# A decoder layer's software pipeline: a new table of stage order per engine and of shared PSUM banks

## What is computed

```python
x = x + _L0_attn_ref(_layernorm(x, axis=-1), L0_attn_W_attn, L0_attn_b_attn, L0_attn_W_proj, L0_attn_b_proj)
x = x + _L0_xattn_ref(ctx_1024, ctx_1024, _layernorm(x, axis=-1), ...)
x = x + _L0_ffn_ref(_layernorm(x, axis=-1), ...)
# attention: softmax(mask(q k^T / sqrt(8))) v, q and k scaled by a rope factor
# ffn:
rw, sel = jax.lax.top_k(softmax(x @ router_w.T), 2)
h = jax.nn.silu(g) * u                  # per expert, F = 256
y = jnp.einsum('etf,efd->etd', h, w_down)
out = jnp.einsum('te,etd->td', cw, y) + gate * shared
```

## Time and profile before

| what | us |
|---|---|
| median of 3 runs | 505.77 (505.45 to 506.39) |
| profiled execution, its own time | 505.77 |
| span of the profiled execution | 503.9 |
| outside the span | 1.87 |
| PE busy | 441.4, 88% of the span |
| DVE busy | 357.6, 71% |
| ACT busy | 294.3, 58% |
| POOL busy | 200.1, 40% |

### The profile page before, as it was taken

How to read it: one execution, slowest core, us unless ns; L and a number is a source line. 1 busy time by engine, 2 the same in 40 slices (tenths; PEclk the granted TensorE clock), 3 DMA queues, 4 the chain that set the end, 5 groups by cost and what they waited for, 6 DMA issues and landing times.

```text
span 503.9 us, 13713 instructions
## 1 busy us (share of the span) xinstructions
PE 441.4 (88%) x4508; PEld 298.5 (59%) x4508; DVE 357.6 (71%) x1236; ACT 294.3 (58%) x951; POOL 200.1 (40%) x247
## 2 busy tenths in 40 slices
PE   4868899999989989999999997678988889989993
PEld 3323555655556556556565555456777777777783
DVE  4573677888888798797886957794666666656585
ACT  1125678878778787778687865521444444444520
POOL 7702030031443432432323255550555555555471
PEclk9999999999999999999999997588999999999998
DMA  7600001101011011111111016121332223221294
GB/s 198 178 13 23 29 9 33 36 29 40 19 51 51 19 50 52 34 51 35 50 45 31 24 56 207 43 82 37 85 82 77 77 76 85 75 79 58 64 345 129
DMA packets 41604, 34.69 MB, mean 69 GB/s; under 512 B 6464, under 2 KB 36432, under 8 KB 41536
## 3 DMA queue, kind: packets, MB, share of 16 engines
q1 hardware_dynamic: 36478, 24.51, 17.1%
q0 software_dynamic: 4320, 8.99, 5.3%
q10 hardware_dynamic: 738, 0.33, 0.2%
HBM read 17.26 MB, written 12.09 MB: 58 GB/s over the span
## 4 chain that ended last, share of the span: by engine, by line
PE 64%; DVE 16%; issue 9%; ACT 5%; another core or an unknown queue 2%; SPq 1%; POOL 1%; DMA 1%; ACTq 0%; DVEq 0%; POOLq 0%
PE ps_scores L855 7%; PE ps_scores L677 6%; PE ps_shared L863 5%; PE ps_scores L706 5%; PE ps_shared L872 4%; PE ps_shared L723 4%; PE ps_shared L660 3%; PE ps_scores L684 3%; PE ps_shared L773 3%; DVE negmax L1158 3%; PE ps_scores L809 3%; PE ps_scores L702 3%; DVE vst L1357 2%; PE ps_scores L711 2%
## 5 line engine op out<-in xcount | busy, mean ns | idle before, releaser
L610 POOL DMA_INDIRECT ys<-ctx_t,xload x71 | 68.7, 968 | 69.4 <-ACT ctx_t L1044 51.0
L949 ACT ACTIVATE probs<-ps_scores 128x512 f32<-128x512 f32 x128 | 69.7, 608 | 14.7 <-PE ps_scores L711 14.7
L597 POOL TENSOR_TENSOR x1b<-x,bias 128x128 f32<-128x128 f32 x32 | 14.4, 450 | 160.6 <-DVE x L1179 160.6
L591 POOL DMA_INDIRECT xs<-xrow,posu x64 | 63.8, 997 | 27.4 <-DVE rsum L1280 13.7
L855 PE MATMUL ps_scores<-wide,xe 128*128 x213 | 68.3, 430 | 0.8 <-DVE xe L1352 0.8
L945 ACT ACTIVATE s_copy<-ps_scores 128x512 f32<-128x512 f32 x64 | 38.4, 605 | 31.5 <-PE ps_scores L684 31.5
L1363 DVE COPY probs<-ps_shared 128x256 f32<-128x256 f32 x71 | 30.1, 424 | 37.6 <-PE ps_shared L863 25.6
L1034 ACT ACTIVATE xe<-ps_scores 128x128 fp32r<-128x128 f32 x71 | 19.8, 278 | 51.0 <-PE ps_scores L847 34.8
L1158 DVE TENSOR_REDUCE negmax<-ps_scores 128x4 f32<-128x512 f32 x64 | 41.3, 685 | 10.5 <-PE ps_scores L684 9.9
L872 PE MATMUL ps_shared<-wd,probs 128*128 x284 | 43.9, 277 | 0.3 <-DVE probs L1363 0.3
L677 PE MATMUL ps_scores<-wide,qk 32*128 32x512 f32 x256 | 38.4, 671 | 2.9 <-ACT probs L949 2.6
(11 more groups left out here) (219 smaller groups left out, 1035.5 us busy)
## 6 DMA issues: line engine op xcount, KB each, us to landing
xload<-xs SPq DMA_DIRECT2D x71, 66.0 KB
wide<-qk SPq DMA_DIRECT2D x64, 64.0 KB
wide<-ys SPq DMA_DIRECT2D x8, 512.0 KB, 8.4
ctx_t<-in_ctx SPq DMA_DIRECT2D x32, 64.0 KB, 1.9
out_x<-res SPq DMA_DIRECT2D x8, 256.0 KB, 3.1
ys<-ctx_t,xload POOLq DMA_INDIRECT x71
wd<-in_L_ffn_w_down SPq DMA_DIRECT2D x8, 128.0 KB, 3.2
xs<-xrow,posu POOLq DMA_INDIRECT x64
```

The costliest lines, as they stand in the source:

```text
L591: pool.indirect_dma_start(out=xs, out_offset=bass.IndirectOffsetOnAxis(ap=posu[:, g % 2, k, u:u + 1], axis=0), in_=xrow[:, g % 2, k, u, :] ...
L610: pool.indirect_dma_start(out=ys, out_offset=bass.IndirectOffsetOnAxis(ap=xload_i[:, i % XL, C + 1:C + 2], axis=0), in_=ybuf[:, i % 4, :], ...
L949: act.activation(probs[:, b % 2, j * HJ:(j + 1) * HJ, :].rearrange("p a t -> p (a t)"), SC[score_bank(("scores_t", b), j)][:], ACT.Exp)\
```

## The change

The tables `ORDER` and `BANK` get other contents, and one wait goes. No stage's own code is changed, except that DVE's statistics of the next group no longer wait for the former ones, which the same engine made (lines behind 1074 have one number less after the change).

```diff
 ORDER = {
     "SP": [
-        ("project", 14, 1, 0),
-        ("turn_x2", 10, None, None),
-        ("project", 16, 0, 0),
-        ("turn_max", 14, None, None),
+        ("project", 26, 1, 0),
+        ("turn_x2", 18, None, None),
+        ("turn_max", 25, None, None),
+        ("project", 27, 0, 0),
...
     "DVE": [
...
+        ("xout", -5, None, None),
+        ("row_max", 1, 1, None),
...
-BANK = {"turn_xprobs": 1, "turn_x": 0, "turn_y": 0, "xproject": 3, "attn_out": 3, "values": 1, "xscores": 3, "turn_ffn": 2, "xout": 2, "turn_max": 2, "project_v": 0, "tall_sums": 1, "router": 2,
+BANK = {"turn_xprobs": 2, "turn_x": 3, "turn_y": 2, "xproject": 0, "attn_out": 3, "values": 3, "xscores": 1, "turn_ffn": 3, "xout": 2, "turn_max": 2, "project_v": 2, "tall_sums": 1, "router": 0,
...
-                w.ge(x_stats, g)
```

More of the change, by code:

```diff
@@ L72 @@
     "PE": [
-        ("scores", -3, None, None),
-        ("turn_ffn", -10, None, None),
-        ("xscores", -8, None, None),
-        ("turn_y", -6, None, None),
-        ("values", -5, None, None),
-        ("xout", -9, None, None),
-        ("turn_x2", -7, None, None),
-        ("scores_t", -4, None, None),
-        ("router", -10, None, None),
-        ("attn_out", -6, None, None),
-        ("project_v", -1, None, None),
-        ("tall_sums", -5, None, None),
-        ("project", 0, 0, 0),
@@ L86 @@
-        ("ranks", -14, None, 0),
-        ("gate_up", -42, None, None),
-        ("xproject", -7, None, None),
-        ("project", 0, 1, 0),
-        ("turn_x", 1, None, 0),
-        ("turn_max", -3, None, None),
-        ("turn_xprobs", -8, None, None),
+        ("turn_max", -5, None, None),
+        ("scores", -4, None, None),
+        ("xout", -10, None, None),
+        ("turn_ffn", -11, None, None),
+        ("xscores", -9, None, None),
+        ("turn_x2", -8, None, None),
+        ("turn_y", -7, None, None),
@@ L93 @@
+        ("values", -6, None, None),
+        ("scores_t", -5, None, None),
+        ("project_v", -2, None, None),
+        ("router", -11, None, None),
+        ("attn_out", -7, None, None),
+        ("gate_up", -42, None, None),
+        ("tall_sums", -6, None, None),
+        ("turn_xprobs", -9, None, None),
+        ("ranks", -15, None, 0),
+        ("turn_x", 0, None, 0),
+        ("xproject", -8, None, None),
+        ("project", -1, 0, 0),
+        ("project", -1, 1, 0),
     ],
     "ACT": [
+        ("rstd_x", 2, None, 0),
@@ L95 @@
+        ("turn_x2", -8, None, None),
+        ("route", -15, None, 0),
+        ("turn_y", -7, None, None),
+        ("values", -6, None, None),
         ("xscores", -9, None, None),
-        ("turn_x2", -8, None, None),
         ("rstd_ffn", -10, None, None),
         ("exps", -5, 0, None),
+        ("project_v", -2, None, None),
         ("exps", -5, 1, None),
-        ("project_v", -2, None, None),
         ("exps", -5, 2, None),
+        ("turn_xprobs", -9, None, None),
         ("exps", -5, 3, None),
@@ L163 @@
 W_LOADS = 15
-BANK = {"turn_xprobs": 1, "turn_x": 0, "turn_y": 0, "xproject": 3, "attn_out": 3, "values": 1, "xscores": 3, "turn_ffn": 2, "xout": 2, "turn_max": 2, "project_v": 0, "tall_sums": 1, "router": 2, "turn_x2": 0, "ranks": 0, "project": (2, 0)}
+BANK = {"turn_xprobs": 2, "turn_x": 3, "turn_y": 2, "xproject": 0, "attn_out": 3, "values": 3, "xscores": 1, "turn_ffn": 3, "xout": 2, "turn_max": 2, "project_v": 2, "tall_sums": 1, "router": 0, "turn_x2": 0, "ranks": 3, "project": (3, 1)}
 def bank_fills():
```

27 lines of the change are left out of this document (10 added, 17 removed).

## The result

| | before | change |
|---|---|---|
| median, us | 505.61 (504.01 to 506.39, 4 runs) | 529.23 (526.58 to 530.22, 4 runs) |
| ratio | | 1.0464 (95%: 1.0417 to 1.0510) |
| profiled execution: time / span, us | 505.77 / 503.9 | 527.34 / 525.6 |
| mean granted TensorE clock of the span | 0.968 | 0.942 |

A forecast was written before the change was run, and what follows sets the result against it. PE was nearest its limit, only its idle time could change, and PE and ACT waiting on each other set plain steps. Span 503.9 + 11.3 (loop) − 3.8 (drain) = 511.4, with 1.87 around it 513.3, stated as 513.5 us; range 499 to 519.

The forecast's parts named there:

- What bounds the kernel: Whole kernel: PE, busy 88%, is nearest its limit; its matmuls stay, so only its idle time can change.
- Plain and remainder 2 steps: Steps 14, 18, 22: 7.95 us against 8.81; step 26 grows by 0.23; together −2.4 us.
- the wait behind `xout`: PE's `turn_y` waits for DVE to drain `xout`: 0.07 us in a step without extras, counting in full.
- the 0.16 among the exps: ACT's `turn_xprobs` between two exps lengthens each step by 0.16 us, to 7.88 where nothing else binds.
- The 0.8 us of step 22: `xproject` waited 0.84 us behind the late `xout` in step 22; this wait vanishes.
- Remainder 0: Steps 12, 16, 20, 24, 28: DVE comes late from the former step; 8.6 us against 8.05 in step 20; +2.7 us.
- Remainder 1: Steps 13, 17, 21, 25: `turn_y` waits 0.93 us if scatters still delay DVE; 9.97 against 9.33; with 29, 30: +4.1 us.
- Remainder 3: Steps 15, 19, 23, 27: route in the middle, 9.50 us against 8.45 in step 23; with step 31, +5.3 us.
- The route: Steps 15, 19, 23, 27: DVE's route takes 2.85 us mid-step; `xproject` on bank 0 waits for the router.
- The drain: After the loop: DVE's 5.0 us block of split weights moves between the last routers; −3.8 us, range −5.0 to 0.
- Behind the drain: Everything after the drain, expert tiles included, whose order is not touched: 0 us.
- Rival A: Scatters no longer delay the steps: loop +3.9, drain −3.8, 505.9 us; chance 0.20.

The follow-up runs named there:

- the five maxima: Five extra DVE maxima with unused results before the drain of `xout` in steps 15, 19 and 23 of the changed kernel: 502.65 us, ratio 1.0432.

## Why the prediction was wrong in size

- **What bounds the kernel.** Right in the main: of the 21.7 us, 16.9 are idle time of PE. But the prediction held that only the idle time can change, and PE's busy time rose by 4.8 us with the same 4508 matmul records, at a mean clock of 0.942 against 0.968.
- **Plain and remainder 2 steps.** Right: 7.98 against 7.95. The split of the 0.26 us was not: the wait behind `xout` is 0.22 us and not 0.07 (it moves line 711 by 0.13), and the 0.16 among the exps measured 0.13. The 0.8 us of step 22 went, as forecast, but two things went at once. `xout` moved ahead, and the two scatters at +2.8 to +5.1 left the step. On chip 13 the kernel before, with these scatters, takes 7.72 us in step 22, so the 0.8 us were late signals. Whether the move of `xout` alone would have removed them is not shown.
- **Remainder 0.** The sum of 2.7 us was right by luck. Steps 16, 20 and 24 take 8.85 us against 8.6, but not because DVE comes late out of the step before: its first maximum starts at +1.56 to +1.59, where the forecast had DVE free at +2.1. A scatter stands at +1.46 to +1.62, and the drain of `xout` behind it waits, in step 20 (start 199.99) by 0.70 us:

```profile
201.59 0.68 DVE L1157 TENSOR_REDUCE negmax<-ps_scores 128x4 f32<-128x512 f32 x1
202.97 0.35 DVE L1211 SCALAR_TENSOR_TENSOR res<-ps_shared,xinv,x1b 128x128 f32<-128x128 f32 x1 [0.70 <-PE ps_shared L773]
```

On chip 13, without late signals, DVE's first maximum comes at +1.78 to +1.91 and the same steps take 8.24 to 8.37.
- **Remainder 1.** Nearly: 9.90 to 9.94 against 9.97 in three of the four steps (9.54 in step 25), with a wait of 737 of 0.82 to 0.85 us for DVE's late drain as described; steps 29 and 30 (8.30, 8.15) were put too high at 8.81. Together 1.8 us too much.
- **Remainder 3.** This step failed. The sum, 9.5 us, let a scatter delay DVE by 0.43 us (the middle of 0 and 0.86) and nothing after that; the steps took 12.80, 12.58 and 14.07. The prediction does not name POOL's normalisation and line 924 at all. It counted the gain in step 22, which the scatters leave, and did not follow them into step 23, where two more stand. There DVE's drain of `xout` came 3.1 us late, beside four scatters in a row, and line 737 waited 3.3 us. The term for TensorE's clock behind such a wait was missing altogether: it fell to 0.59 to 0.76. Stall and clock together are 11.0 of the 14.2 us that the forecast lacks. That a late drain and the clock behind it make such a step is shown by the five maxima; that the bunched scatters are what made it late is argued.
- **The route.** Its length came out well: without the stall the step takes 9.06 us (rival A gave 9.07), and the two steps without POOL's normalisation 9.39 and 9.77. The place of the wait did not. `xproject` (755) does not wait for the router on bank 0. It is `ranks` (790) that waits, just ahead of it: its bank, 0 before the change, is now 3, behind `attn_out`, which DVE drains (1178) behind route and router. Step 15 on chip 13, start 146.97:

```profile
155.21 0.19 PE L790 MATMUL ps_shared<-selb,tri 128*128 128x32 bf16 x1 [0.98 <-DVE x L1178]
...
155.30 0.47 PE L755 MATMUL ps_shared<-xcT,wA 128*128 128x128 f32 x2
```

- **The drain.** Half right: the block of 5.0 us went, but the drain's last steps wait for each other (line 779 for DVE's 1195 for 1.54 us at 341.86) and it gained 1.5 us, not 3.8: 2.3 us of the error.
- **Behind the drain.** 2.1 us more in the changed kernel, costed at nothing. Of it 1.6 lie between the first product of the shared expert and the first scatter of an expert tile. On chip 13 this stretch takes 156 to 157 us for both kernels. The cause stays open.
- **Rival A** (no delay by scatters) came true on four of six chips, but not with its 505.9 us: there both kernels lose their late heads. Its lengths of the steps fit chip 13: 9.07 against 9.06, 9.11 against 9.14, 7.95 against 7.98 in step 29. The change is 2.1% slower there (490.49 against 481.39), close to the forecast's 1.5% by luck, since the late heads that the forecast counted with do not exist there; with the loads in two batches or the normalisation put back it is 1.5 to 2% slower on chips 10, 4 and 11.

## What to carry to other kernels

When an instruction moves in a hand-written order, follow its queue: what stands behind it on the engine moves too, and where it lands may be worse than what it left. A long TensorE wait is to be priced with the slower matmuls that may stand behind it: here they added up to 1.7 us to waits of 1.5 us, up to 2.7 to 1.9 us, and up to 2.6 to 3.0 us, and in other steps of the same executions nothing or little. In a table tuned as a whole, single entries put back are not "the old kernel in part": of six such edits of the change two made no difference and four a slower kernel, since each stage's bank and neighbours fit the new place of the others.

## What the runs showed of the hardware

- Chips of one type differ, or differed when they were measured. Of six, two had late signals; the kernel before takes 505 to 508 us on those and 481 to 482 us on the others, 5% apart. In the 71 expert tiles, each with one scatter, the stretch from the first to the last scatter takes 119.6 to 122.4 us on the one kind and 102.4 to 102.6 on the other, for both kernels alike: 0.24 to 0.28 us per tile. For the kernel before, these tiles (17.2 us) and steps 6 to 30 (209.7 against 202.8 us) make the whole difference between the first chip and chip 13.
- On the two chips ACT's copy, where a scatter of POOL runs when it should start, comes 0.4 to 1.0 us after the scatter's end (before: +2.50 for a scatter that ended at +1.61; the kernel with route and `turn_x2` moved: +2.47 for +2.07). With scatters in a row it comes later still, and the signal need not fall under one: in step 23 of the change `scores` ended at 228.24, between two scatters (to 228.12 and from 228.77), and the copy came at 230.36, behind the latter, which ended at 229.76. DVE's drain came at 232.08, the last scatter having ended at 231.04.
- The granted clock after a stall of one length isn't always the same: 0.51 and 0.76 behind two waits of 3.0 us, and 0.60 and 1.00 behind two of 1.9 us in all. So the time of such a step scatters by up to 2.7 us within one execution.
